# Chunk 0's head products as 32-bit matmuls, and a later rounding of its head weights

## What is computed

```
base   = x @ W.T                                   # 512 -> 512
logits = x @ Wr.T + 5 * onehot(language id)        # 8 experts
two highest logits -> softmax -> gates (8, six of them zero)
h      = x @ A.T                                   # 8 experts x rank 16 = 128 columns
lora   = (h * gates) @ B                           # 128 -> 512
out    = x + base + 2 * lora
```

## Time and profile before

| | us |
|---|---|
| median of three runs | 79.92 (79.78 to 81.01) |
| the profiled execution's own time | 79.51 |
| its span, from the first to the last instruction | 77.7 |
| TensorE busy | 74.3 (96%) |
| VectorE busy | 48.3 (62%) |
| ScalarE busy | 22.4 (29%) |
| GpSimd busy | 22.4 (29%) |

### The profile page before, as it was taken

The page is one execution under the profiler, slowest core; times in us unless marked ns, Lnnn a source line. Parts: engine busy times, 40 slices in busy tenths (PEclk is TensorE's granted clock), DMA queues, the critical chain, the costliest instruction groups (busy, mean ns, idle before and its releaser), DMA issues.

```text
span 77.7 us, 1632 instructions
## 1 busy us (share of the span) xinstructions
PE 74.3 (96%) x505; PEld 70.6 (91%) x505; DVE 48.3 (62%) x220; ACT 22.4 (29%) x57; POOL 22.4 (29%) x26
## 2 busy tenths in 40 slices
PE   5999999999999999999999999999999999999960
PEld 2369999999999999999999999999999999999950
DVE  0097678879855739283855739283855739787750
ACT  1654931523403223140504023141404023122100
POOL 4054724156160605133060605033050606000000
DMA  1999993498379199999930000450000072032043
GB/s 10 307 372 360 413 414 161 57 408 353 45 297 424 47 234 436 422 278 345 410 161 16 0 0 0 196 209 0 0 0 0 0 304 101 0 135 104 35 139 135
DMA packets 4037, 14.24 MB, mean 183 GB/s; under 512 B 448, under 2 KB 1472, under 8 KB 3776
## 3 DMA queue, kind: packets, MB, share of 16 engines
q1 hardware_dynamic: 3744, 13.65, 47.8%
q10 hardware_dynamic: 288, 0.53, 1.8%
HBM read 9.99 MB, written 4.19 MB: 182 GB/s over the span
## 4 chain that ended last, share of the span: by engine, by line
PE 96%; DVE 1%; issue 0%
PE heads_ps L436 44%; PE base_ps L436 28%; PE warm_ps L509 5%; PE heads_ps L476 5%; PE base_ps L476 5%; PE base_ps L480 2%; PE heads_ps L480 2%; PE ghT_ps L467 2%; PE base_ps L460 2%; DVE out_sb L428 1%; PE warm_ps L467 0%
## 5 line engine op out<-in xcount | busy, mean ns | idle before, releaser
L209 POOL TENSOR_TENSOR x_lo<-xT_sb,x_hi 128x512 fp32r<-128x512 f32 x14 | 18.1, 1296 | 38.2 <-ACT x_hi L244 36.7
L436 PE MATMUL heads_ps<-w_hi,x_hi 128*128 128x392 f32 x64 | 22.6, 364 | 0.0
L436 PE MATMUL heads_ps<-w_hi,x_lo 128*128 128x392 f32 x64 | 21.1, 342 | 0.0
L436 PE MATMUL heads_ps<-w_lo,x_hi 128*128 128x392 f32 x64 | 21.1, 340 | 0.0
L436 PE MATMUL base_ps<-w_hi,x_lo 128*128 128x256 f32 x60 | 16.7, 281 | 0.0
L436 PE MATMUL base_ps<-w_hi,x_hi 128*128 128x256 f32 x60 | 16.4, 284 | 0.0
L436 PE MATMUL base_ps<-w_lo,x_hi 128*128 128x256 f32 x60 | 16.3, 281 | 0.0
L301 DVE TENSOR_TENSOR ghT_lo<-ghT_ps,ghT_hi 128x128 fp32r<-128x128 f32 x15 | 4.4, 291 | 14.9 <-ACT ghT_hi L248 14.8
L436 PEld LDWEIGHTS heads_ps<-w_hi,x_hi 128*128 128x128 f32 x64 | 12.0, 192 | 0.9 <-ACT x_hi L234 0.5
L248 ACT ACTIVATE ghT_hi<-ghT_ps 128x128 fp32r<-128x128 f32 x15 | 4.1, 275 | 29.5 <-PE ghT_ps L467 29.5
L436 PEld LDWEIGHTS heads_ps<-w_lo,x_hi 128*128 128x128 f32 x64 | 11.8, 189 | 0.0
(11 more groups left out here) (51 smaller groups left out, 98.9 us busy)
## 6 DMA issues: line engine op xcount, KB each, us to landing
x_sb<-in_x SPq DMA_DIRECT2D x4, 768.0 KB, 5.7
out<-out_sb SPq DMA_DIRECT2D x4, 768.0 KB, 5.0
xT_sb<-in_xT SPq DMA_DIRECT2D x3, 768.0 KB, 4.4
xT_sb<-in_xT SPq DMA_DIRECT2D x1, 1024.0 KB, 6.5
x_sb<-in_x SPq DMA_DIRECT2D x1, 1024.0 KB, 11.8
first_sb<-in_first SPq DMA_DIRECT2D x2, 454.0 KB, 5.4
out<-out_sb SPq DMA_DIRECT2D x2, 256.0 KB, 2.1
out<-out_sb SPq DMA_DIRECT2D x4, 128.0 KB, 1.8
```

The source lines that it names most:

```text
L209: nc.gpsimd.tensor_tensor(x_lo[:, s, :], xT_sb[:, t - len(FIRST), :], x_hi[:, s, :].bitcast(FP32), ALU.subtract).then_inc(x_lo_made, 1)
L436: return nc.tensor.matmul(dst, xs[:, s, chunks[k]], ws[:, k, cols], start=(k == 0 and n == 0), stop=(k == KC - 1 and n == last_n))
```

## The change

The warm-up gets two matmuls fewer. For chunk 0 of the first two tiles, the six head products on rounded operands are replaced by two matmuls, one for each tile, whose operands are x and the head weights as they landed, in plain 32 bits. They wait for the two landings alone. ScalarE no longer rounds the base weights of chunk 0; VectorE does it, as its first step. VectorE rounds the head weights of chunk 0, which tile 2 and all later tiles still need, behind the lower parts of chunk 1. TensorE gets a wait for them ahead of tile 2. The counts of the semaphores shift to match.

```diff
--- before.py
+++ after.py
@@ -25,7 +25,7 @@
 SLOTS = 3
 LANG_BIAS = 5.0
 SCALING = 2.0
-WARM_UP = 9
+WARM_UP = 7
 WIDTH = HEADS + BASE
 
 
@@ -111,6 +111,9 @@
         ident_made = sem("ident_made")
         expert_made = sem("expert_made")
         bias_made = sem("bias_made")
+        wb0_hi_made = sem("wb0_hi_made")
+        w0_lo_made = sem("w0_lo_made")
+        wh0_lo_made = sem("wh0_lo_made")
         wh_hi_made = sem("wh_hi_made")
         w_hi_made = sem("w_hi_made")
         w_lo_made = sem("w_lo_made")
@@ -257,8 +260,6 @@
                           first[:, 1, 0:FIRST_X + IDS + HEADS]).then_inc(chunk_landed[0], 16)
             act.wait_ge(x_landed, 16)
             chunk_upper(0)
-            act.wait_ge(wb_landed, 16)
-            w_upper(0, base_cols)
             for k in range(1, KC):
                 act.wait_ge(chunk_landed[k - 1], 16)
                 chunk_upper(k)
@@ -368,24 +369,27 @@
             def heads_upper(k):
                 nc.vector.tensor_copy(w_hi[:, k, heads_cols], w_sb[:, k, heads_cols]).then_inc(wh_hi_made, 1)
 
-            dve.wait_ge(wh_landed, 16)
-            heads_upper(0)
-            dve.wait_ge(wh_hi_made, 1)
-            w_lower(0, heads_cols)
-            dve.wait_ge(w_hi_made, 1)
-            w_lower(0, base_cols)
+            dve.wait_ge(wb_landed, 16)
+            nc.vector.tensor_copy(w_hi[:, 0, base_cols], w_sb[:, 0, base_cols]).then_inc(wb0_hi_made, 1)
+            dve.wait_ge(wb0_hi_made, 1)
+            nc.vector.tensor_tensor(w_lo[:, 0, base_cols], w_sb[:, 0, base_cols], w_hi[:, 0, base_cols].bitcast(FP32),
+                                    ALU.subtract).then_inc(w0_lo_made, 1)
             dve.wait_ge(expert_made, 1)
             dve.wait_ge(x_landed, 16)
             nc.vector.tensor_scalar(bias[:, :], expert[:, :], ids_sb, LANG_BIAS, ALU.is_equal,
                                     ALU.mult).then_inc(bias_made, 1)
             dve.wait_ge(chunk_landed[0], 16)
             heads_upper(1)
+            dve.wait_ge(wh_hi_made, 1)
+            w_lower(1, heads_cols)
+            dve.wait_ge(w_hi_made, 1)
+            w_lower(1, base_cols)
+            heads_upper(0)
             dve.wait_ge(wh_hi_made, 2)
-            w_lower(1, heads_cols)
-            dve.wait_ge(w_hi_made, 2)
-            w_lower(1, base_cols)
+            nc.vector.tensor_tensor(w_lo[:, 0, heads_cols], w_sb[:, 0, heads_cols],
+                                    w_hi[:, 0, heads_cols].bitcast(FP32), ALU.subtract).then_inc(wh0_lo_made, 1)
             for k in range(2, KC):
-                dve.wait_ge(w_hi_made, k + 1)
+                dve.wait_ge(w_hi_made, k)
                 w_lower(k, heads_cols)
                 w_lower(k, base_cols)
             dve.wait_ge(b_hi_made, 1)
@@ -509,33 +513,31 @@
                     nc.tensor.matmul(warm_ps[:, :], ones, ones_moving, start=True, stop=True)
 
             warm(WARM_UP)
+            pe.wait_ge(x_landed, 16)
+            pe.wait_ge(wh_landed, 16)
+            for t in FIRST:
+                nc.tensor.matmul(heads_ps[t][:, 0:HEADS], first_x[0][:, t, :], w_sb[:, 0, heads_cols],
+                                 start=True, stop=False)
             pe.wait_ge(chunk_hi_made, 1)
-            pe.wait_ge(wh_hi_made, 1)
-            for t in FIRST:
-                heads_product(t, 0, 0)
-            pe.wait_ge(w_hi_made, 1)
+            pe.wait_ge(wb0_hi_made, 1)
             for t in FIRST:
                 base_product(t, 0, 0)
             pe.wait_ge(chunk_lo_made, 1)
             for t in FIRST:
-                heads_product(t, 0, 2)
                 base_product(t, 0, 2)
-            pe.wait_ge(w_lo_made, 1)
-            for t in FIRST:
-                heads_product(t, 0, 1)
-            pe.wait_ge(w_lo_made, 2)
+            pe.wait_ge(w0_lo_made, 1)
             for t in FIRST:
                 base_product(t, 0, 1)
             for k in range(1, KC):
                 pe.wait_ge(chunk_hi_made, k + 1)
                 if k == 1:
-                    pe.wait_ge(wh_hi_made, 2)
+                    pe.wait_ge(wh_hi_made, 1)
                 else:
-                    pe.wait_ge(w_hi_made, k + 1)
+                    pe.wait_ge(w_hi_made, k)
                 for t in FIRST:
                     heads_product(t, k, 0)
                 if k == 1:
-                    pe.wait_ge(w_hi_made, 2)
+                    pe.wait_ge(w_hi_made, 1)
                 for t in FIRST:
                     base_product(t, k, 0)
                 if k == 1:
@@ -550,18 +552,19 @@
                     if k < KC - 1:
                         for t in FIRST:
                             base_product(t, k, 2)
-                pe.wait_ge(w_lo_made, 2 * k + 1)
+                pe.wait_ge(w_lo_made, 2 * k - 1)
                 for t in FIRST:
                     last = heads_product(t, k, 1, last_n=1)
                     if k == KC - 1:
                         last.then_inc(heads_done, 1)
-                pe.wait_ge(w_lo_made, 2 * k + 2)
+                pe.wait_ge(w_lo_made, 2 * k)
                 for t in FIRST:
                     base_product(t, k, 1)
                     if k == KC - 1:
                         base_product(t, k, 2).then_inc(base_done, 1)
 
             pe.wait_ge(x_hi_made, 1)
+            pe.wait_ge(wh0_lo_made, 1)
             for k in range(KC):
                 for n in range(2):
                     heads_product(2, k, n)
```

## The result

The changed kernel takes 80.36 us (80.11 to 81.62, ten runs), the kernel before 79.77 us beside it (79.51 to 81.01, ten runs). The ratio is 1.0057, 95% interval [1.0036, 1.0078]: 0.45 us slower, and clear of noise. The prediction was 79.9 and no change; the value lies inside its range of 79.3 to 80.9, but the time moved, and to the side that was not forecast. The profiled execution took 80.36 with a span of 78.4, against 79.51 and 77.7. A few executions of either kernel take over 1 us more; the ratios leave them out.

The account below looks back on a forecast made before the run. TensorE was taken as the bound, 96% of the chain. Removing 0.85 us of warm-ups was offset by two more streams, less low-clock cover, and 0.28 lead-in: -0.03, taken as zero; VectorE's steps cost nothing. Forecast 79.9 us, range 79.3 to 80.9.

Parts of the forecast that it names:

- its first: Start of the kernel: the change touches only what precedes 8.5 us; TensorE's gain or loss by chunk 2 carries through unchanged.
- The clauses on VectorE: VectorE's new order up to chunk 2: three extra steps cost nothing, with 0.35 us of cover at chunk 2.
- Rival C: VectorE late at chunk 2: three extra steps overrunning their 0.35 us cover by 0.3 give 80.2; chance 0.05.
- The sum: TensorE's work through chunk 0: ends at 6.84 instead of 6.87, a net of -0.03 us, taken as zero.
- rival A: 32-bit head products of chunk 0 dearer because loads are not hidden: 80.6 to 82.1; chance 0.20.
- dearest form: All eight loads of the 32-bit products exposed: +2.2 us, 82.1; 0.03 of the rival's 0.20 chance.
- The 32-bit product is four streams: Chunk 0's head products: each takes four streams with hidden loads, 0.71 us at the high clock level, 1.31 at the low.
- Chunk 2's landing caps the gain: Chunk 2's first load on TensorE: it can come no more than about 0.1 us earlier, whatever is saved before.
- Rival D: 32-bit products of chunk 0 cheaper, one stream each: heads end at 4.86, but chunk 2 caps it: 79.8; chance 0.07.
- Rival B: TensorE's clock: the pause before the 32-bit products delays its rise from 5.3 to 8.7, +1.7 us, 81.6; chance 0.08.
- the pause at 3.93: TensorE after seven warm-ups: it waits there for the landings of chunk 0 before the 32-bit products.

Follow-up runs that it names:

- e9: Kernel before with one memset of an existing 8-column buffer at VectorE's start: 80.36 us, ratio 1.0047.
- e5: Changed kernel with GpSimd's subtractions of chunks 2 and 3 of the first two tiles cut to 8 columns: 80.31 us, ratio 1.0046.
- e11: Changed kernel with one memset at VectorE's start and no new buffer: 80.06 us, ratio 1.0011.
- e12: Kernel before with an extra cast and subtraction on VectorE, written into output rows overwritten later, no new buffer: 79.95 us, ratio 1.0011.
- e6: Changed kernel with tile 2's three head products of chunk 0 also made by one 32-bit matmul: 80.86 us (two runs), ratio 1.0131.
- e2: Kernel before with TensorE's part of the change alone (seven warm-ups, two 32-bit products): 79.96 us, ratio 0.9993.
- e4: Changed kernel with nine warm-ups again instead of seven: 80.47 us, ratio 1.0074.
- e3: Kernel before with a spare cast and subtraction on VectorE into a new buffer behind chunk 1's lower parts: 80.24 us, ratio 1.0038.
- e10: Kernel before with two memsets of existing buffers at VectorE's start: 79.89 us, ratio 1.0003.
- e15: Kernel before with four memsets of small buffers at VectorE's start, one execution for the profile: 79.84 us.
- e14: Kernel before with three memsets of small buffers at VectorE's start, one execution for the profile: 81.14 us.
- e16: Kernel before with a new one-column buffer ahead of the gate buffers and two memsets on VectorE: 80.31 us, ratio 1.0046.
- e7: Changed kernel with a memset of a new one-column buffer as VectorE's first instruction: 80.37 us, ratio 1.0072.
- e1: Changed kernel with the lower part of chunk 0's head weights made by GpSimd instead of VectorE: 80.84 us, ratio 1.0120.
- e8: TensorE's part of the change on the kernel before, with chunk 2's head weights rounded by VectorE instead of ScalarE: 80.24 us, ratio 1.0045.
- e13: e8 with one memset added at VectorE's start: 79.97 us, ratio 0.9998.

## Why the prediction was wrong

**The step that failed** is its first: "The change touches only what lies before 8.5 us, so everything is decided there". It took the change for the work it moves. But it also makes VectorE's program one instruction longer, and at that length VectorE stops for 0.43 us ahead of the last `gh`, 65 us later. That costs 0.27 us of TensorE in the profile, and 0.47% (0.37 us, interval 0.12 to 0.64) as e9 measures it, of the 0.57% (0.45 us) of the change. What the rest is, if there is one, the intervals do not tell. No row of before could have priced it: the earlier trace rows shows the chain on TensorE at that place. What could have been said is that a small edit changes the length of every program it touches, and that the last tile's `gh` has little cover: it came 0.38 us later, and TensorE lost 0.27.

**The clauses on VectorE** were wrong too, though little hangs on them. I summed 1.04 + 0.36 + 1.05 and allowed a start at 8.65; it was 8.80. Then I let chunk 2's lower parts take their 0.90. They took 1.44, for GpSimd's x_lo of chunk 3 ran beside them, and I asked only when the head part is wanted, not the base part, for which TensorE waited at 10.29. Rival C had the place and nearly the size (0.3 against 0.36) at a chance of 0.05. The runs show when it counts: only where chunk 2 lands early. ScalarE starts on chunk 2 at 7.16 in the profile of before; in e5, e11 and e12 it starts at 7.57 to 7.86, and VectorE waits there. That fits the profile's 0.36 beside a median's 0.1% (e11, e12), which is itself not told from nothing.

**Two terms of the working.** The sum let chunk 0 end at 6.84, with 3.3 streams at the low level until 5.3. It ended at 6.48 in the profile (6.08 + 0.40), because the clock was up from the first stream on; the landing of chunk 2 hid that. And rival A's dearest form took 0.53 for a stream with its load exposed at the high level, where its own prices give 0.178 + 0.19 = 0.37; so it comes to about 81.2, not 82.1. No run met it.

**What held.** The 32-bit product is four streams: 0.71 forecast, 0.66 measured (e6). Its loads are hidden, so rival A falls. Chunk 2's landing caps the gain of TensorE at 0.1: in the changed kernel 8.39 against 8.38, and e2 at 0.9993. Rival D was not met. Rival B falls: the pause at 3.93 did not put the clock's rise off. In the profile after, the 32-bit rows are 0.33 long from the first on, so TensorE was at 2.4 GHz at 4.2, right behind the warm-ups; and e4 with nine warm-ups shows the same (four rows in 1.48 us). The moment scatters: 5.3 in the profile of before, about 6.6 in e3's, both with nine warm-ups; behind 6.7 in e6's with seven; in no profile does it come near the 8.7 of rival B. What B said of the price is right where chunk 2 lands early: in e3 the rise came some 1.3 us later than before, and TensorE was 0.66 behind at tile 2.

**One landing sets most of the scatter.** The start of ScalarE's rounding of x of chunk 2, against the span, one execution each:

| kernel | chunk 2 | stop | span | 77.7 + (chunk 2 - 7.16) + 0.27 for a stop |
|---|---|---|---|---|
| before | 7.16 | no | 77.7 | 77.7 |
| e10 | 7.13 | no | 77.7 | 77.7 |
| e9 | 7.47 | yes | 78.3 | 78.3 |
| e15 | 7.53 | no | 78.0 | 78.1, yet no landing in its chain: the clock rose late |
| e5 | 7.57 | yes | 78.4 | 78.4 |
| e11 | 7.74 | no | 78.3 | 78.3 |
| e2 | 7.78 | no | 78.3 | 78.3 |
| e12 | 7.86 | no | 78.4 | 78.4 |
| e4 | 8.66 | yes | 79.4 | 79.5 |
| e14 | 8.81 | no | 79.3 | 79.4 |
| changed | 7.22 | yes | 78.4 | 78.0, and 0.36 of VectorE's lateness |
| e16 | 7.16 | no | 78.0 | 77.7, and 0.27 for moved buffers |
| e3 | 7.42 | no | 78.6 | 78.0; not the landing: the late clock, and moved buffers |
| e7 | 8.61 | no | 79.4 | 79.2, and 0.27 for moved buffers |
| e1 | 8.50 | no | 79.8 | 79.0, and 0.7 of wait at the first transpose |
| e6 | 8.68 | yes | 79.5 | 79.5 |
| e8 | 7.42 | yes | 78.2 | 78.2 |
| e13 | 7.78 | no | 78.4 | 78.3, though its chain starts from a late chunk 1 |

The five executions of this table that took over 81 us (e1, e4, e6, e7, e14) are the five in which chunk 2 came at 8.50 or later. e3 and e15 show the second source of scatter: where the clock rises late and chunk 2 is early, the clock sets the start.

A kernel bound by one load shows its neighbours' edits only when that load comes early. The pair of profiles I had, 7.16 and 7.22, was such a case, so it laid half of the loss on VectorE's queue; the medians lay most of it on the stop.

What stays open: why the stop comes at this one length, and what it is. The Trainium skill ("Runtime: NRT & Kernel Launch", Instruction fetch mechanics) says that each engine fetches its program in blocks ahead of use and that crossing a block is mostly hidden. No run here shows that the stop is such a fetch. Nor was it tried whether other engines' programs have such a place.

## What to carry to other kernels

When an edit of a well filled kernel moves the time by half a per cent, put one idle instruction into the kernel before, and two, and take them out again, ahead of any story about the moved work; the same for a small buffer. Compare two profiles by their late landings first: what one early execution shows as a wait may be hidden in most. And give VectorE and GpSimd's subtractions different times; run beside each other, one waits for up to the other's whole duration.

## What the runs showed of the hardware

- VectorE stood still for 0.43 us, inputs ready, at one instruction of its program, in six of six profiles with a program one longer than before, and in none of twelve at 0, 2, 3 or 4 more.
- A one-column buffer allocated ahead of the gate buffers (4 bytes for each partition) made each tile 0.02 to 0.03 us longer (4.385 against 4.36), 0.46% in all.
- Two-operand subtractions of VectorE and GpSimd exclude each other: 0.57 became 1.08 us, a pair of 0.90 became 1.44 and 1.95, and a cast of two columns took 0.67 instead of 0.17, ending 0.03 behind GpSimd's subtraction.
- The granted clock reads 1.00 where matmuls run at half pace: the pace of rows (0.65 or 0.33 for the same row) told the level, the column did not.
- TensorE's rise to the full level came anywhere from before 4.2 to behind 6.7 us in executions of nearly the same program; a rise 1.3 us later cost 0.66 us where nothing hid it (e3).
